# A selective-scan block with a mixture of experts: one state's product and sum moved to VectorE in PSUM, the opening and the two ends of the order rewritten

## What is computed

```python
dA = jnp.exp(dts[..., None] * A[None, None])
dBu = dts[..., None] * Bm[:, :, None, :] * hs_ble[..., None]
state = a * state + bu
y = jnp.einsum('ben,bn->be', state, c)
```

## Time and profile before

| | |
|---|---|
| median of 3 runs | 1367.48 us (1365.01 to 1369.09) |
| the profiled execution | 1367.53 us, its span 1365.7 us |
| PE, PEld busy | 1312.0 us (96%), 1233.5 us (90%) |
| DVE busy | 1242.2 us (91%) |
| ACT busy | 1193.1 us (87%) |
| POOL busy | 1243.7 us (91%) |
| transfers | 170.76 MB, 125 GB/s |

### The profile page before, as it was taken

How to read it: one execution, slowest core, us unless ns; L and a number is a source line. 1 busy time by engine, 2 the same in 40 slices (tenths; PEclk the granted TensorE clock), 3 DMA queues, 4 the chain that set the end, 5 groups by cost and what they waited for, 6 DMA issues and landing times.

```text
span 1365.7 us, 26543 instructions
## 1 busy us (share of the span) xinstructions
PE 1312.0 (96%) x9314; PEld 1233.5 (90%) x9314; DVE 1242.2 (91%) x1644; ACT 1193.1 (87%) x1990; POOL 1243.7 (91%) x625
## 2 busy tenths in 40 slices
PE   2599999999999999999999999999999999999998
PEld 2589999999999999999999999999999999999987
DVE  4598989999899999999999899999989999998987
ACT  3889899889889988999899989989998999988984
POOL 2789999999989999999999999999999999999996
PEclk9899999999999999999999999999999999999999
DMA  6544344534434544444444434434443444434442
GB/s 167 153 133 122 118 130 126 129 115 128 128 113 127 140 121 122 127 119 122 124 125 129 123 114 123 144 115 129 121 124 115 130 131 127 121 119 118 124 133 70
DMA packets 184533, 170.76 MB, mean 125 GB/s; under 512 B 42672, under 2 KB 167632, under 8 KB 184400
## 3 DMA queue, kind: packets, MB, share of 16 engines
q1 hardware_dynamic: 150608, 121.86, 30.7%
q10 hardware_dynamic: 33792, 47.20, 12.1%
HBM read 163.72 MB, written 5.24 MB: 124 GB/s over the span
## 4 chain that ended last, share of the span: by engine, by line
PE 53%; DVE 16%; POOL 12%; ACT 9%; issue 9%; ACTq 1%; SPq 0%; DMA 0%; DVEq 0%; POOLq 0%
PE pair_ps L849 22%; PE out_ps L967 12%; PE front_ps L849 7%; POOL state L468 6%; DVE state L750 5%; PE turn_ps L929 5%; PE out_ps L977 3%; ACT decay L546 3%; DVE acc L757 3%; POOL state L477 3%; POOL moe L483 2%; DVE u L767 2%; ACT L546 2%; DVE dt L738 2%; DVE moe L774 1%
## 5 line engine op out<-in xcount | busy, mean ns | idle before, releaser
L750 DVE TENSOR_TENSOR_SCAN state<-decay,state 128x512 f32<-128x512 f32 x512 | 615.0, 1213 | 70.6 <-ACT decay L546 67.4
L468 POOL TENSOR_TENSOR state<-du,b_rep 128x1024 f32<-128x1024 f32 x256 | 639.2, 2505 | 29.0 <-DVE u L767 28.9
L546 ACT ACTIVATE decay<-dt,neg_a 128x255 f32<-128x255 f32 x1024 | 437.2, 467 | 39.6 <-DVE state L750 27.2
L967 PE MATMUL out_ps<-w_down,moe 128*128 128x256 f32 x1536 | 353.0, 379 | 0.1
L483 POOL TENSOR_TENSOR moe<-moe,rw_rep 128x512 f32<-128x512 f32 x192 | 285.9, 1492 | 45.8 <-DVE moe L774 36.5
L967 PEld LDWEIGHTS out_ps<-w_down,moe 128*128 128x128 f32 x1536 | 283.1, 190 | 34.6 <-issue 0.5
L849 PE MATMUL pair_ps<-xnT_hi,w_up_hi 128*128 128x256 f32 x768 | 228.7, 298 | 8.9 <-ACT moe L554 8.7
L477 POOL TENSOR_TENSOR state<-state,c_rep 128x1024 f32<-128x1024 f32 x96 | 228.6, 2382 | 2.7 <-DVE state L750 2.7
L546 ACT ACT_TABLE_LOAD x176 | 225.8, 1283 | 3.1
L849 PE MATMUL pair_ps<-xnT_hi,w_gate_hi 128*128 128x256 f32 x768 | 223.2, 291 | 0.6 <-DVE moe L774 0.5
L849 PE MATMUL pair_ps<-xnT_hi,w_up_lo 128*128 128x256 f32 x768 | 217.6, 283 | 0.0
(11 more groups left out here) (112 smaller groups left out, 2055.2 us busy)
## 6 DMA issues: line engine op xcount, KB each, us to landing
w_down<-in_L_ffn_w_down_dram SPq DMA_DIRECT2D x384, 128.0 KB, 2.6
b_rep<-b_dram ACTq DMA_DIRECT2D x128, 256.0 KB, 3.4
rw_rep<-rw_dram SPq DMA_DIRECT2D x256, 96.0 KB, 2.6
rw_rep<-rw_dram SPq DMA_DIRECT2D x256, 64.0 KB, 2.7
c_rep<-b_dram ACTq DMA_DIRECT2D x96, 128.0 KB, 3.1
rw_rep<-rw_dram SPq DMA_DIRECT2D x256, 32.0 KB, 2.5
x_in<-L_attn_input_states_dram SPq DMA_DIRECT2D x16, 256.0 KB, 3.5
res<-L_attn_input_states_dram SPq DMA_DIRECT2D x16, 256.0 KB, 4.1
```

What stands on the lines that cost most here:

```text
L468: pool.tensor_tensor(state[:, n % STATES, :, :], du2[:, q, :, :], b_rep[:, n // BCH % 2, n % BCH, :][:, None, :].broadcast_to([P, ET, T]), ...
L546: last = act.activation(decay[:, h, j, 1:T], dt[:, q, e, 1:T], ACT.Exp, scale=neg_a[:, e, n:n + 1])
L750: dve.tensor_tensor_scan(x, decay[:, h, :, :].rearrange("p e t -> p (e t)"), x, 0.0, ALU.mult, ALU.add).then_inc(scanned, 1)
L967: last = pe.matmul(out_ps[:, c, :], moe[:, p % RING, j, c * P:(c + 1) * P], w_down[:, p % RING, j, :], start=(p == 0 and j == 0 and c == 0 ...
```

## The change

- State 7 goes from `BY_TURN` to `BY_ROW`, and it alone is in `ROWS_BY_VECTOR`. VectorE scans it over its own decays in PSUM (`scan`), multiplies each half there by C's row (`row_product`) and adds it to `u2` (`add_half`). TensorE turns 9 states, GpSimd multiplies 6 as before. The decays of state 8 wait for the sums instead of the scan, and ScalarE writes again the zero that stands at the border of two channel tiles. `c_rep` takes 7 rows per block instead of 6, over the same 2 buffers.
- `normed` goes from VectorE to ScalarE; VectorE computes a 128x2 shift for it (`shifted`). The router's last product (L726) goes from VectorE to ScalarE (`share`).
- In block 0 the front uses the two halves of `turn_ps` beside `front_ps` (`front_bank`), so that `hid1`, the logits, `lowT` and `dt1` need not wait for a reader. Logits and router weights leave the chain of `FRONT` and get semaphores of their own.
- `w_in` is split by columns instead of rows: its hidden half is piece 0, its gate half piece 13.
- Every table has three versions, for block 0, blocks 1 to 14 and block 15 (`stage`). One row of one table stands in the diff.

```diff
-    BY_ROW = [n for n in range(NS) if n in ((2, 4, 6, 8, 10, 12))]
+    BY_ROW = [n for n in range(NS) if n in ((2, 4, 6, 7, 8, 10, 12))]
...
-    FRONT = ["xnT", "hid0", "hid1", "logits", "weightsT", "low", "lowT", "dt0", "dt1"]
-    BY_SCALAR = [name for name in FRONT if name not in ("xnT", "logits")]
+    FRONT = ["xnT", "hid0", "hid1", "low", "lowT", "dt0", "dt1"]
+    ROUTER = ["logits", "weightsT"]
+    BY_SCALAR = FRONT[1:]
...
+    def stage(i):
+
+        return 0 if i == 0 else 2 if i == BLOCKS - 1 else 1
+
+    UNIT_AT = [[-31, -22, -17, -3, 1, 19, 21, 34, 35, 53, 59, 62, 62, 65, 65, 75, 82, 88, 100, 100, 104, 106, 117, 120],
...
+    C_LOAD_AT = [[-17, 31, 39, 45, 52, 57, 68], [-25, -10, 30, 41, 60, 60, 90], [-18, 9, 40, 45, 61, 67, 84]]
+    ROWS_BY_VECTOR = [n for n in BY_ROW if n in ((7,))]
+    ROW_SUMS = sorted(BY_ROW, key=lambda n: n if n in ROWS_BY_VECTOR else n + ROW_LAG)
...
+        w_in_rows = w_in_d.rearrange("(k p) e -> p k e", p=P)
+        splits = [(w_in[0][:, :, 0:E], w_in[1][:, :, 0:E], w_in_rows[:, :, 0:E])]
...
+        GATE_SPLIT = 1 + (WGROUPS - 1) * 2 * HT
+        splits.insert(GATE_SPLIT, (w_in[0][:, :, E:2 * E], w_in[1][:, :, E:2 * E], w_in_rows[:, :, E:2 * E]))
...
+        def front_bank(i, name):
+
+            if i == 0 and name in ("hid1", "lowT", "dt1"):
+                return turn_ps[:, 0, :].rearrange("p (j t) -> p j t", j=2)
+            if i == 0 and name in ROUTER:
+                return turn_ps[:, 1, :].rearrange("p (j t) -> p j t", j=2)
+            return front_ps
...
+        def wait_summed(eng, i, k, h=1):
+
+            if k < 0:
+                eng.wait_ge(skip_ready, i + 1)
+            elif ROW_SUMS[k] in ROWS_BY_VECTOR:
+                eng.wait_ge(row_summed, row_half(i, ROW_SUMS[k], h))
+            else:
+                eng.wait_ge(row_added, row_at(i, ROW_SUMS[k]))
...
-                    if before in BY_ROW:
+                    if before in ROWS_BY_VECTOR:
+                        pool.wait_ge(scanned, half_at(at, before, 1))
+                    elif before in BY_ROW:
...
+                k = i * NR + r
+                if k >= ROWS:
+                    row_multiplied(act, (k - ROWS) // NR, BY_ROW[(k - ROWS) % NR])
...
-                if not (isinstance(i, int) and i == 0 and n == 0):
-                    act.wait_ge(scanned, half_at(i, n - 1, h))
+                before, of = (n - 1) % NS, i if n > 0 else i - 1
+                if before in ROWS_BY_VECTOR and of >= 0:
+                    act.wait_ge(row_summed, row_half(of, before, h))
+                    act.activation(decay[:, h, 1, 0:1], dt[:, q, 2 * h, 0:1], ACT.Copy, scale=0.0)
+                elif of >= 0:
+                    act.wait_ge(scanned, half_at(of, before, h))
...
+            def share(i):
+
+                act.wait_ge(rw_step, 3 * i + 3)
+                if i > 0:
+                    act.wait_ge(weights_filled, i)
+                for c in range(TT):
+                    last = act.activation(rw[:, c, :], rest[:, c, :], ACT.Copy, scale=inv[:, c:c + 1])
+                last.then_inc(rw_ready, 1)
+
+            def normed(i):
+                act.wait_ge(shift_ready, i + 1)
+                for c in range(TT):
+                    last = act.activation(x_in[:, c, :], x_in[:, c, :], ACT.Identity, bias=shift[:, c:c + 1], scale=rstd[:, c:c + 1])
+                last.then_inc(xn_ready, 1)
...
-            def normed(i):
+            def shifted(i):
                 dve.wait_ge(rstd_ready, i + 1)
-                for c in range(TT):
-                    last = dve.tensor_scalar(x_in[:, c, :], x_in[:, c, :], moments[:, c, 0:1], rstd[:, c:c + 1],
-                                             ALU.subtract, ALU.mult)
-                last.then_inc(xn_ready, 1)
+                dve.scalar_tensor_tensor(out=shift[:, :], in0=moments[:, :, 0], scalar=-1.0, in1=rstd[:, :],
+                                         op0=ALU.mult, op1=ALU.mult).then_inc(shift_ready, 1)
...
-                dve.tensor_tensor_scan(x, decay[:, h, :, :].rearrange("p e t -> p (e t)"), x, 0.0,
-                                       ALU.mult, ALU.add).then_inc(scanned, 1)
+                a = decay[:, h, :, :].rearrange("p e t -> p (e t)")
+                dve.tensor_tensor_scan(a if n in ROWS_BY_VECTOR else x, a, x, 0.0, ALU.mult, ALU.add).then_inc(scanned, 1)
...
+            def row_product(i, n, h):
+
+                r = i * NR + BY_ROW.index(n)
+                dve.wait_ge(scanned, half_at(i, n, h))
+                dve.wait_ge(c_loaded[r % ROWS], (r // ROWS + 1) * 16)
+                x = decay[:, h, :, :]
+                dve.tensor_tensor(x, x, c_rep[:, r % ROWS, :][:, None, :].broadcast_to([P, 2, T]), ALU.mult).then_inc(row_ready[1], 1)
+
+            def add_half(i, q, n, h):
+
+                wait_summed(dve, i, ROW_SUMS.index(n) - 1, h)
+                row_multiplied(dve, i, n, h)
+                x = u2[:, q, 2 * h:2 * h + 2, :]
+                dve.tensor_tensor(x, x, decay[:, h, :, :], ALU.add).then_inc(row_summed, 1)
...
-                        if first_pair(i):
-                            wait_split(pe, HT)
-                    else:
+                        if i == 0:
+                            pe.wait_ge(split[0], 1)
+                    elif i > 0:
                         pe.wait_ge(taps_done, 2 * i + 1)
```

336 lines of the change are left out of this document (210 added, 126 removed).

## The result

The changed kernel takes 1379.15 us (median of 4 runs, 1378.00 to 1380.59), beside 1368.28 for the kernel before on the same chip: a ratio of 1.0086, 95% interval 1.0072 to 1.0100. It is slower by 11 us. The forecast was 1349 us.

What follows compares the result with a forecast made beforehand. PE (TensorE) was taken as the bound. 1367.5 - 12.6 (transposes) + 1.2 (changes of product kind) + 1 (new waits) - 8 (opening) = 1349.1, rounded to 1349 us; range 1339 to 1358, widened to 1337 to 1361.

Steps and rivals of the forecast that it cites:

- What bounds the kernel: Middle blocks: PE, busy 80.52 of 81.00 us, sets the pace; the three other engines have 4.5 to 8 us to spare.
- TensorE's 0.71 us a block: Each block: state 7's transposes leave PE, 12.6 us less 1.2 for more changes of product kind, net 11.4 us.
- The first rival: Middle blocks: another engine takes PE's place, the period stays at 81.3 us; 1359.5 us in all, chance 0.12.
- VectorE: Each block: removed and added work net -0.6 us, leaving 76.2 us of work in 80.5; costed at nothing.
- The page against the row: Normalizing products on VectorE: 0.935 us each by the row, 0.19 by the skill's page; the sum went by the row.
- ScalarE: Each block: 1.9 us added at most, giving 75.1 us of work in 80.5, hidden beside PE.
- The new wait: State 8's decays wait for VectorE's sums; VectorE finds them ready; PE's new waits 1 us in 15 blocks, between 0 and 8.
- The slower rival: Each block: state 8's first scan waits for its decays, VectorE becomes the bound; 82.7 us a block, 1381 us, chance 0.08.
- The opening: Start and block 0: earlier hid0, second taps and silu, less 2.5 us given back; gain 8 us, bounds 3 and 13.
- The end: After the last scans: chain unchanged, 0 us, between -3 and +3.

Runs made afterwards that it cites:

- shift_gpsimd: The changed kernel with the 128x2 shift made by GpSimd in two products instead of by VectorE; 1363.58 us, ratio to before 0.9968.
- before_less_tensor: The kernel before with 6 of the 8 transposes of state 9 left out in every block; nothing changed, the interval of the ratio begins at 0.9988.
- less_vector: shift_gpsimd with VectorE's sum of state 7's first half cut from 256 to 16 columns of each tile; worth nothing against shift_gpsimd's 1363.6 us.
- shift_products: The changed kernel with the shift still on VectorE, but as two plain products of 128x2; 1405.71 us, ratio to before 1.0276.
- norm_back: The changed kernel with x normalized on VectorE again, two instructions in the shift's slots, ScalarE's two left out; 1407.09 us.

## Why the prediction was wrong

- **What bounds the kernel.** Here the argument failed. It read PE's 80.52 busy us in 81 as "PE sets the pace" and gave TensorE's 0.71 us a block "all of it on the path". The path is the step that failed. The size of the term can only be seen roughly. Blocks 2 to 12 of the kernel before, of the changed kernel and of shift_gpsimd (the row is as in the earlier trace rows):

```profile
240.10:1135.77 895.67, 891.41 (x6405) 841.44 (x6404) 843.40 (x1124) 807.84 (x1354) 840.97 (x419) 1.00 0.43 125
...
238.95:1146.54 907.59, 889.96 (x6316) 831.81 (x6315) 844.21 (x1124) 825.72 (x1420) 824.11 (x418) 1.00 0.42 124
...
235.02:1132.56 897.54, 881.90 (x6317) 823.13 (x6316) 838.24 (x1112) 824.88 (x1420) 828.60 (x441) 1.00 0.44 126
```

PE's recorded time is 0.86 us a block less in shift_gpsimd than before, near the forecast 0.71, but only 0.13 less in the changed kernel, whose PE list is the same as shift_gpsimd's: recorded busy time is not work alone. A cut of like size shows what it was worth. In before_less_tensor 0.6 us of TensorE's time, at state 9, was worth nothing already in the kernel before. By that, 11.4 us of the 18.4 forecast were never there; the same cut at state 7 was not made. The first rival (PE's freed time not won) had this at 0.12. The row against it was in hand: VectorE, ScalarE and GpSimd each at 73 to 76.5 us, with VectorE waiting for decays.

- **VectorE.** The products and sums were sized at 0.672 and measured 0.697 and 0.687. Overwriting the decays costs the scan 1.22 for 1.21. The step that failed is the half sentence in which "the small router product that leaves and the small shift that comes stand against each other". The shift measured 1.17 us, and moving it to GpSimd gave back 0.92 us of period and 2.9 us of block 0, 15.6 us in all. VectorE's time as such is not what it costs, as far as one cut can say: less_vector took 0.5 us out of VectorE's list at state 7 and gained nothing. The net of -0.6 us a block for VectorE did not come either: by the rows above it recorded 76.7 us a block before and 76.7 in the changed kernel. With the shift gone the middle is 81.59 beside 81.42: the rest of the change is close to nothing there.
- **The page against the row.** The prediction took 0.935 us for a normalizing product from its row against an estimate of 0.19 from the Trainium skill's page "VectorE: DVE Perf Modes" (section "The TRN2 errata"). The row's mean hid what it was made of: at 714.34 us the pair took 1.89 us beside a GpSimd instruction of 2.36 from 713.39, so the first waited till about 715.8 and the second ran in 0.4. That 0.4 is the least of the line, still twice the estimate. It was the same wait that the shift got. Removing the pair and putting the shift in its place freed the work and kept the wait.
- **ScalarE** took 24.2 us in 16 blocks, 1.5 each (forecast 1.9 at most), costed at nothing behind PE. PE was no cover. In the new order the price is small all the same, since shift_gpsimd, which has this work, stays within 0.2 us of before's period; in before's order the normalizing with its shift cost 4.0 us a period.
- **The new wait.** Forecast: VectorE finds state 8's decays ready. It does: in blocks 1 to 14 state 8's first scan starts with no idle time before it, and the waits for the decays of all states in 800 us are 33.6 us where they were 42.0. ScalarE waits 6.9 us in all for the sums in front of its zeros.
- **The slower rival** gave 82.7 us a period and 1381 us; measured are 82.51 and 1379. Its number came true by luck, and its mechanism didn't. Waits for state 8's decays did not grow; the shift and its wait for GpSimd's instruction did it. It had 0.08.
- **The opening.** Forecast 8, block 0 gave 4.4. The silu came at 22.89 (forecast 23.2) and the first scan at 45.24 (45 to 48); both were right. Then block 0 took 109.4 us from first scan to final addition instead of 104.4. 2.9 of these 5.0 us are the shift, which stood 2.28 us behind GpSimd there. In shift_gpsimd block 0 ends 7.3 us earlier than before, close to the 8; but block 1 takes 83.28 where it took 81.03, so that 5.1 us are left at its end.
- **The end.** Forecast 0 between -3 and +3; blocks 14 and 15 are -1.6 together.

From the kernel before to shift_gpsimd the last addition moves by -4.5 us: block 0 -7.3, block 1 +2.3, blocks 2 to 12 +1.9, block 13 +0.4, blocks 14 and 15 -1.8. The shift on VectorE then adds 14.9. What stays open is which chain holds the period at 81.4 to 81.6. Shorter decays of state 9 on ScalarE shorten it, before the change and after. Open too is whether the shift cost its 0.92 us through VectorE's list or through the wait of ScalarE, whose normalized x TensorE needs. Not tried were a cut at another state, and a shift on VectorE that ScalarE doesn't wait for.

## What to carry to other kernels

A full engine is not yet the bound: when four engines stand between 90 and 99% in a stretch, take half a microsecond out of one in each round (leave a part of the computation out, at more than one place if you can) before pricing a change by its time. A tiny instruction is not a cheap one; look at least, median and most of its line, and at what the neighbour engine runs in the same moment. Where a small VectorE instruction on SBUF stands directly behind a GpSimd result, give that last step to GpSimd; an operand in PSUM might do as well, which was not tried for the shift. And a piece put back into an order made without it is not priced by that: each of the two put back here cost some 2 us a block.

## What was not expected of the hardware

VectorE instructions of 2 elements took 0.16 us with GpSimd idle and up to 2.29 with it busy, ending with GpSimd's instruction. Of two such in a row (shift_products), and of two on 256 elements (norm_back), each waited for an instruction of its own. Statistics of x (one SBUF operand) kept 0.40 to 0.42 us and the zero 0.06 beside a busy GpSimd. The wait goes the other way as well: while a row sum of VectorE ran from 721.08 to 723.05 in norm_back, the product of GpSimd that began at 721.92 took 2.28 us instead of 1.28.
